# The routing of a top-2 expert layer moved ahead of its stage, and four stage beginnings put in another order, in a kernel of four transformer layers

## What is computed

```python
x = x + L0_xattn(layernorm(x), ctx)   # 16 heads of 8
x = x + L0_ffn(layernorm(x))          # 8 experts, argmax of 8 router scores, GELU, F = 512
x = x + L1_xattn(layernorm(x), ctx)   # 16 heads of 64
x = x + L1_ffn(layernorm(x))          # dense, piecewise linear GELU
x = x + L2_xattn(layernorm(x), ctx)   # self attention, GELU block, cross attention, GELU block
x = x + L2_ffn(layernorm(x))          # 8 experts, top 2:
...
logits = silu(xt @ rw1 + rb1) @ rw2 + rb2
_, idx = top_k(logits, 2)
w = softmax(where(mask_of(idx), logits, -inf))
h = silu(einsum('nd,edh->enh', xt, we1) + be1)
y = xt + einsum('ne,end->nd', w, einsum('enh,ehd->end', h, we2) + be2)
...
x = x + L3_xattn(layernorm(x), ctx)   # 16 heads of 8
x = x + L3_ffn(layernorm(x))          # 8 experts, argmax, GELU
```

## Time and profile before

| what | us |
|---|---|
| median of 3 runs (lowest, highest) | 1477.28 (1472.34, 1477.69) |
| profiled execution: its time, its span | 1477.49, 1475.7 |
| PE busy, share of the span | 1002.4, 68% |
| PEld (weight loads) | 753.7, 51% |
| DVE | 906.7, 61% |
| ACT | 696.9, 47% |
| POOL | 621.5, 42% |
| DMA | 71.57 MB, mean 49 GB/s |

### The profile page before, as it was taken

One profiled execution on the slowest core, in us unless ns is written; L12 is line 12 of the kernel. 1 busy time (PEld: TensorE's weight loads), 2 busy tenths in 40 slices (PEclk: granted clock), 3 DMA queues, 4 the chain that ended last, 5 costly groups with the idle time before them and its releaser, 6 DMA issues.

```text
span 1475.7 us, 37422 instructions
## 1 busy us (share of the span) xinstructions
PE 1002.4 (68%) x14883; PEld 753.7 (51%) x14940; DVE 906.7 (61%) x2386; ACT 696.9 (47%) x1404; POOL 621.5 (42%) x575
## 2 busy tenths in 40 slices
PE   1477578679898463678887478958259674567664
PEld 0355367446677243356664256735147462455554
DVE  4567554677775794788975567746244255766532
ACT  3556345565554432654526356645135354455321
POOL 3456723164353332364541355621440417556232
PEclk9778688889999675788987769968569795778787
DMA  6433222110010100000001000000212114431122
GB/s 198 132 95 108 69 68 63 40 40 24 23 31 10 34 17 32 19 16 10 3 3 36 1 2 3 4 2 1 69 37 72 42 36 115 137 111 44 48 73 72
DMA packets 68792, 71.57 MB, mean 49 GB/s; under 512 B 11599, under 2 KB 51919, under 8 KB 68431
## 3 DMA queue, kind: packets, MB, share of 16 engines
q1 hardware_dynamic: 64528, 60.78, 14.3%
q0 software_dynamic: 4096, 8.40, 1.8%
HBM read 44.91 MB, written 23.59 MB: 46 GB/s over the span
## 4 chain that ended last, share of the span: by engine, by line
PE 44%; DVE 22%; ACT 11%; issue 10%; POOL 6%; DMA 3%; POOLq 2%; SPq 1%; another core or an unknown queue 1%; ACTq 0%; DVEq 0%
PE psum L651 16%; PE psum L1132 6%; PE psum L1150 6%; DVE area L1742 4%; PE psum L773 2%; ACT xn L1243 2%; PE psum L813 2%; ACT area L1221 2%; PE psum L658 2%; DVE area L1862 2%; POOL sorted_in L2606 2%; DVE stats L1723 1%; POOLq L2416 1%; POOL area L2524 1%; DVE area L1848 1%
## 5 line engine op out<-in xcount | busy, mean ns | idle before, releaser
L1221 ACT ACTIVATE area<-psum 128x512 bf16<-128x512 f32 (+4 forms) x278 | 144.8, 541 | 239.6 <-PE psum L813 138.6
L1742 DVE TENSOR_TENSOR area<-psum,area 128x512 bf16<-128x512 f32 (+3 forms) x270 | 159.9, 620 | 58.1 <-ACT area L1221 52.0
L2335 DVE TENSOR_TENSOR area<-area 128x512 bf16<-128x512 f32 x106 | 73.7, 698 | 143.3 <-ACT area L1638 99.7
L2477 POOL TENSOR_TENSOR area<-area 77x1024 bf16<-77x1024 f32 x64 | 119.9, 1890 | 79.2 <-ACT area L1354 79.2
L1132 PE MATMUL psum<-xT_hi,moe 128*128 128x128 bf16 x848 | 114.6, 237 | 27.7 <-issue 23.7
L1150 PE MATMUL psum<-moe,area 128*128 x1272 | 110.9, 229 | 26.9 <-issue 25.9
L658 PE MATMUL psum<-wide,xn 128*128 128x128 f32 x144 | 32.7, 372 | 120.4 <-ACT xn L1243 108.4
L1354 ACT ACTIVATE area<-psum 77x1024 f32<-77x1024 f32 (+1 forms) x96 | 92.7, 1017 | 31.3 <-PE psum L773 31.3
L1150 PEld LDWEIGHTS psum<-moe,area 128*128 128x128 bf16 x1272 | 86.4, 102 | 40.9 <-issue 31.0
L2435 POOL TENSOR_TENSOR moe<-stage,moe 128x512 bf16<-128x512 f32 x47 | 55.6, 1183 | 120.7 <-ACT moe L1216 120.5
L1132 PEld LDWEIGHTS psum<-xT_hi,moe 128*128 x848 | 83.3, 107 | 37.2 <-issue 30.8
(11 more groups left out here) (245 smaller groups left out, 3010.2 us busy)
## 6 DMA issues: line engine op xcount, KB each, us to landing
area<-keys_dram SPq DMA_DIRECT2D x24, 320.0 KB, 4.8
area<-sorted_in SPq DMA_DIRECT2D x22, 256.0 KB, 3.4
sorted_out<-area SPq DMA_DIRECT2D x22, 256.0 KB
keys_dram<-area SPq DMA_DIRECT2D x8, 640.0 KB, 2.9
stage<-in_w_L0m SPq DMA_DIRECT2D x16, 256.0 KB
stage<-in_w_L2m SPq DMA_DIRECT2D x16, 256.0 KB
stage<-in_w_L3m SPq DMA_DIRECT2D x16, 256.0 KB
area<-queries_dram SPq DMA_DIRECT2D x24, 128.0 KB, 2.5
```

The source lines that it names most:

```text
L1221: ins = act.activation(out, bank, ACT.Copy)
L1742: ins = dve.tensor_tensor(out, bank, high, ALU.subtract)
L2335: dve.tensor_tensor(R.HL[u], R.HF[u], upper(R.HF[u]), ALU.subtract).then_inc(K.tile_split, tiles.one())
L2477: pool.tensor_tensor(A.PL[n % 4][0:A.L], A.PF[n % 4][0:A.L, :].rearrange("p (h q) -> p h q", h=8), A.PH[n % 4][0:A.L], ALU.subtract).then_ ...
```

## The change

Areas. VX and the maxima lie elsewhere in Dense's area, `VX_words` is the same memory as VX in words of 4 bytes, and the sorted rows of the late half lie behind the area of the results. `begun` says how many groups of an attention have their statistics from the stage in front: 2 in L1x and L3x, 1 in L0x, 0 in L2a1 and L2a2. `then` of L0m and L2m is now the attention behind them; `add_at`, `moments_at` and `shift_at` are tiles of the Routed loop.

```diff
+LATE_ROWS_AT = {1: OWN_AT + 2 * HB * D + 320, 2: OWN_AT + 2 * HB * D}
...
+        self.begun = 2 if late is not None else 0
...
+        self.begun = 2 if late is not None else 1
...
+        values = [words(GB * DENSE_TILES * 72) for _ in range(2)]
+        self.VX = [v.bitcast(BF16).rearrange("p (a n) -> p a n", a=2) for v in values]
+        self.VX_words = values
+        self.NM = [words(64, BF16) for _ in range(2)]
+        self.ON = [words(128).rearrange("p (h d) -> p h d", h=H) for _ in range(2)]
+        self.OT = words(128, BF16).rearrange("p (a n) -> p a n", a=2)
...
-        self.tiles = [K.carve(at, NT * D).rearrange("p (t d) -> p t d", d=D) for at in (AREA - D - NT * D, 0)]
+        self.tiles = [K.carve(at, NT * D).rearrange("p (t d) -> p t d", d=D)
+                      for at in (AREA - D - NT * D, LATE_ROWS_AT[k])]
+
+        self.then = None
+        self.add_at, self.moments_at, self.shift_at = (2 * NT - 8, 2 * NT - 4), 2 * NT - 3, 2 * NT - 1
```

```diff
         before, after = A.first_jobs()
+        if A.begun:
+            group_turned(0)
...
+        group_turned(0)
         project_keys(0)
-        group_turned(0)
...
-            if N.then is not None and g == 3:
-                for r in (0, 1):
-                    tokens_turned(N.then, r)
-        if N.then is not None:
-            for r in (0, 1):
+        for half in range(HALVES if N.then is not None else 0):
+            for r in (2 * half, 2 * half + 1):
+                tokens_turned(N.then, r)
+            for r in (2 * half, 2 * half + 1):
                 router_hidden(N.then, r)
-            for r in (0, 1):
+            for r in (2 * half, 2 * half + 1):
                 logits(N.then, r)
-            sort_half(N.then, 0)
+            sort_half(N.then, half)
...
-        if R.k == 2:
-            for g in (2, 3):
-                tokens_turned(R, g)
-            for g in (2, 3):
-                router_hidden(R, g)
-            for g in (2, 3):
-                logits(R, g)
-            sort_half(R, 1)
+        load_experts(0)
```

```diff
+    def table_loaded(fn):
+
+        i = stages.n
+        act.activation(K.table_of[:, i:i + 1], K.col("half"), fn)
...
+        normed(K.L0x.name, K.L0x.residual, 0)
...
-            sem.wait_ge(K.results_saved[1], A.late.saved)
+        table_loaded(ACT.Exp)
...
+            elif A.late is not None:
+                sem.wait_ge(K.results_saved[1], A.late.saved)
...
+        if A.begun:
+            group_turned(0)
...
+        group_turned(0)
         keys_hi(0)
+        head_rows(0)
+        queries_hi(0)
         repeat_keys(0)
-        head_rows(0)
-        normed(name, A.residual, 0)
         for t in range(1, 4):
             head_rows(t)
-        group_turned(0)
-        queries_hi(0)
...
+        table_loaded(ACT.Gelu)
...
-            if N.then is not None and g == 3:
-                for r in (0, 1):
-                    tokens_normed(N.then, r)
-                sem.wait_ge(K.affine_split, N.affine0 + NG)
-                for r in (0, 1):
-                    tokens_turned(N.then, r)
             for n in K.loads_of(name, g):
                 split_weights(n)
         if N.then is not None:
             for r in (0, 1):
-                router_hidden(N.then, r)
-            for r in (2, 3):
                 tokens_normed(N.then, r)
+            sem.wait_ge(K.affine_split, N.affine0 + NG)
+            for half in range(HALVES):
+                for r in (2 * half, 2 * half + 1):
+                    tokens_turned(N.then, r)
+                for r in (2 * half, 2 * half + 1):
+                    router_hidden(N.then, r)
+                if half == 0:
+                    for r in (2, 3):
+                        tokens_normed(N.then, r)
+            gates()
...
+        table_loaded(R.act_fn)
...
-        if R.k == 2:
-            for g in (2, 3):
-                tokens_turned(R, g)
-            for g in (2, 3):
-                router_hidden(R, g)
-            gates()
-        else:
+        if R.k == 1:
             tokens_normed(R, 3)
+        if R.b1 is not None:
+            load_experts(0)
...
+        if R.then is not None:
+            normed(R.then.name, R.then.residual, 0)
```

```diff
+        sem.wait_ge(K.load_first, 16)
+        first = norm_stats(K.L0x.residual, 0)
...
+        shift_of(0, first)
+        spread_masks(K.L0x)
...
-        g_stats(0)
         before, after = A.first_jobs()
+        if A.begun:
+            number["x", 1] = second_norm[name]
+            group_turned(0)
...
+        if A.begun < 2:
+            g_stats(1)
...
-            sem.wait_ge(K.values_zeroed, A.order + 1)
+            sem.wait_ge(K.values_zeroed, 2 * A.order + u + 1)
...
-                sem.wait_ge(K.values_zeroed, A.order + 1)
+                sem.wait_ge(K.maxima_zeroed, A.order + 1)
...
-        spread_masks()
-        g_stats(0)
+        group_turned(0)
         keys_lo(0)
         mask_keys(0)
-        shift_of(0, number[0])
-        group_turned(0)
         queries_lo(0)
...
-            for r in (0, 1):
-                route(N.then, r)
+            route(N.then, 0)
             for r in (2, 3):
                 shift_of(r, routed_norm[N.then.name, r])
+            route(N.then, 1)
             sort_half(N.then, 0)
+            for r in (2, 3):
+                route(N.then, r)
+            sort_half(N.then, 1)
+            gates()
...
-        if R.k == 2:
-            route(R, 2)
-            route(R, 3)
-            sort_half(R, 1)
-            gates()
...
-            if tile == HALVES * NT - 1:
-                for g in range(NG // HALVES):
-                    add_own(R, g)
+            if tile in R.add_at:
+                add_own(R, R.add_at.index(tile))
+            if R.then is not None and tile == R.moments_at:
+                sem.wait_ge(K.own_added, own_added.n)
+                number["first"] = norm_stats(K.x, 0)
+                second_norm[R.then.name] = norm_stats(K.x, 1)
+                if R.k == 2:
+                    spread_masks(R.then)
+            if R.then is not None and tile == R.shift_at:
+                shift_of(0, number["first"])
```

```diff
+        rstd(slice(0, 128), group(0))
...
-            pool.memset(A.NM[u], 0.0)
-            ins = pool.memset(A.VX[u].rearrange("p a n -> p (a n)"), 0.0)
-        ins.then_inc(K.values_zeroed, 1)
-        rstd(slice(0, 128), group(0))
+            ins = pool.memset(A.NM[u], 0.0)
+        ins.then_inc(K.maxima_zeroed, 1)
+        for u in range(2):
+            pool.memset(A.VX_words[u], 0.0).then_inc(K.values_zeroed, 1)
         prepare_sort(A.then)
         if A.late is not None:
...
+            if b < B and b % GB == 0:
+                late_values_lo(b // GB)
             if A.late is not None and b == 0:
                 gather(A.late, 3)
-            if b < B and b % GB == 0:
-                late_values_lo(b // GB)
...
+        if R.then is not None:
+            rstd(slice(0, 128), group(0))
+            rstd(slice(0, 128), group(1))
```

```diff
+        keys_away(0)
+        queries_away(0)
+        keys_back(0)
+        queries_back(0)
...
+    K.L0m.then, K.L2m.then = K.L1x, K.L3x
```

134 lines of the change are left out of this document (69 added, 65 removed).

## The result

The changed kernel takes 1429.89 us, the median of 4 runs (1424.11 to 1433.95), the kernel before 1474.81; the ratio is 0.9695 (95% interval 0.9650 to 0.9739). 1430 was forecast. Beside the experiments the same pair gave 1432.61 against 1477.8 (0.9697, 0.9671 to 0.9724), and on another chip 1431.32 against 1478.93 (0.9684, 0.9663 to 0.9705). The profiled execution took 1429.39, its span is 1427.6.

A forecast was written before the change was run, and what follows sets the result against it. No engine bounds it; twelve serial stages, each behind a border where every engine waits, do. Terms -16.7 - 13.0 - 10.2 - 6.8 - 3.6 - 0.8 + 3.9 = -47.2 from the profiled 1477.49 us gave 1430; range 1414 to 1447.

The forecast's parts named there:

- L2f2 to L2m: Border into L2m: second half's routing moves beside L2f2's scatter, second scatter starts at the border; -16.7 us, bounds -9 and -20.
- the lesser of the two shifts, that of the scatter: L2m's start: gain taken from the second scatter's earlier issue, 14.2 us, rather than from the first expert product's shift.
- Rival B: L2m's expert loop is not held by the scatter and runs on; another 11 us go, 1419 us; chance 0.08.
- 20 us of it under 22 us of cover: L2f2's end: 20 us of second-half routing fits beside GpSimd's 22 us scatter, with none of it on GpSimd.
- routing in L2f2 outlasted the scatter: Sign of being wrong: in L2f2 the moved routing ends later than GpSimd's scatter; no size given.
- rival A: L2f2's routing starves beside the scatter; the border gives 5 us instead of 16.7, 1442 us; chance 0.12.
- L2m to L3x: Border into L3x: border 2.9 us sooner, shorter starting chain and memsets, GpSimd's gathers decide; -13.0 us, bounds -8 and -16.
- keeps its length: L3x: add_own(3) behind GpSimd's gathers still takes 8.92 us.
- Start to L0x: Start and L0x's beginning: start some 2 us longer, first scores at 39.8 instead of 50.04; -10.2 us, bounds -7 and -13.
- rival D: Whole kernel slower: denser work lowers TensorE's granted clock; a mean of 0.73 gives 1490 us; chance 0.02.
- L0m to L1x: L1x's start: first maxima at 282.8 instead of 290.19, GpSimd's gathers early; -6.8 us, bounds -4 and -8.
- Tables: ScalarE's table loads moved to stage starts: three attentions give -3.6 us, three feed-forwards 0.8 more; bounds 0 and -6.

The follow-up runs named there:

- e2: Changed kernel with the second half's routing put back behind L2m's border: 1440.83 us.
- e5: Kernel before, unchanged, traced again: 1472.86 us, one run; its second theory was that something of the change, kept when L0x's old order returns, lengthens L0x's loop.
- e6: Changed kernel with VX cleared as bf16 again instead of f32 words: 1440.04 us.
- e7: Changed kernel with L1x not begun in L0m (L1x normalises its first group itself, early statistics taken out): 1444.8 us.
- e8: Changed kernel with every L2m tile using expert 0's weights and biases at a constant address: 1415.93 us.
- e3: Changed kernel with start and L0x put back into the order of before, L3x as changed: 1444.55 us.
- e4: Changed kernel without the small activations that load ScalarE's table at a stage's start: 1437.82 us.
- e10: Changed kernel with sort preparation moved behind gather(3) and the second VX cleared by VectorE in L3x: 1432.29 us.
- e9: Changed kernel run again unedited, as base for later runs on the same chip: 1431.32 us.

## Why the prediction came out right, and where its steps did not

**L2f2 to L2m (-16.7, and 2.9 of the next).** Measured -17.8 for both stages. The scatter of L2f2 starts 3.0 us sooner (2.5 forecast), the second scatter starts at the border, the first product comes at 4.8 (5). The tenth tile of the expert loop stands 38.0 us behind the border instead of 53.2, by VectorE's splits in the timelines: 15.2 to the forecast's 14.2; e2 puts it back to 53.2. Taking "the lesser of the two shifts, that of the scatter" was the decision that mattered. It was right on two of three chips. On the third TensorE is not held, and by the forecast's own working 15.5 us (20.5 less 5) would come; the kernel before has no trace there, so that is argued and not shown. Rival B's mechanism, a loop that the scatter doesn't hold, is real on one chip of three. Whether the holding on the other two is a wait of the kind that the rule quoted at rival B denies, no run tells.

The step that failed is the cover: "20 us of it under 22 us of cover" takes the routing to be as fast beside the scatter as in the open. From `route` to the last gate it took 13.0 us in the open (before, e5, e2) and 18.9 to 22.6 us in the ten traces that have it beside the scatter on these chips. In nine of the ten VectorE's drain is the last at the border, 0.4 to 3.9 us behind GpSimd's; "routing in L2f2 outlasted the scatter" was one of the forecast's signs of being wrong. That is where L2f2 fell short: 76.2 and 76.4 us with the routing 0.4 late, which is the forecast's -2.5, and 78.4 with it 2.6 late. So rival A's mechanism is real, and its price (11.7 us over the forecast) was not paid, since the cover was nearly long enough.

**L2m to L3x (-13.0).** First scores come 9.9 us sooner, the gathers end 9.7 sooner relative to the border and at 28.8 us of it (28.4 by the forecast's sum). L3x gains 13.1 where 10.1 were expected: 11.1 at the first exponentials (35.5 to 24.5) and the rest in the loop. One step that failed is that add_own(3) behind it, 8.92 us, "keeps its length": it took 6.68, 6.58 and 5.07 in the three traces. By e6 each microsecond of the gathers is worth 1.0 to 1.3 in the stage. The rest of the excess is within what the stage varies by: e7 and e8 have the same L3x and took 154.1 and 152.9. The memset at 0.85 ns a value was right: 0.86 for f32.

**Start to L0x (-10.2).** The beginning went as worked out: first scores at 16.4 us of the stage (15.3 forecast), start 1.7 longer (2 forecast). e3, which undoes it, costs 11.9 in the median and 9.8 in the stages. Against the traces of before, only 3.4 were to be seen. Of the 6.8 missing, 1.3 are that the first weights landed later in the three traces of the changed kernel (first copy at 14.5 on average against 13.2), 0.5 the beginning, and 5.0 L0x's loop. That is a step that the forecast did not have: L0x's loop runs at whatever clock TensorE is granted, and that differs between executions. Of twelve traces of kernels with a change in them, three at 0.81 have loops of 109.6 to 110.3 us, nine at 0.72 to 0.76 have 111.6 to 113.4; the two of before had 0.79 and 0.83 and 107.8 and 108.6. The loop of e3, with the old beginning, is long too (112.8 at 0.74), so the new order at the beginning is not what lengthens it. The clock explains some 2.5 us. Beside the three at 0.81 the two loops of before are still about 1.5 us shorter; why, no run settles (theory 2 of e5 is open), nor why the clock was low in nine of twelve. Of rival D, that denser work lowers the clock, there is no sign in the whole span: 0.804 against 0.798. In this one loop it is not excluded. The forecast's argument against D, that the lowest clocks stand in the stretches with little work, rests on L3x's start (0.51); L0x's start of before, as idle, had 0.98 and its busy middle 0.74.

**L0m to L1x (-6.8).** First maxima at 11.7 to 13.1 us (12 forecast), first exponentials 9.8 sooner (36.0 to 26.2); e7 gives 7.7 of these to early normalising and leaves 2.1 to the table and what else leads up to them. Both terms were a little small, by 0.9 each.

**Tables (-3.6 and -0.8).** The sum is near (e4: 5.2 in the median), its parts are not. L2a2 gains 2.5, L2a1 0.4, L1f and L2f1 nothing. The forecast let the load run behind the border, in ScalarE's wait; in the traces it runs ahead of the border, without the wait of the activation that needs it. So it costs nothing there.

**L0m and L3m begin later (+3.9).** Measured +1.5 in all; the first products stand 1.1 us further from the border in each. The step "the table (1.5) stands ahead of it" is wrong for that same reason; the register load remains.

So the forecast hit 1430 by luck as well, because errors cancelled: start and L0x gave 6.8 us less than their term, L2f2 and L2m 2.1 less, the feed-forwards 1.0 less; L3x gave 3.0 more, L1x 1.8, L2a1 and L2a2 0.5, and the late beginnings cost 2.4 less. The other half of the luck is the kernel before, whose median lay at 1474.8 with one more run.

## What to carry to other kernels

Work that a border holds back is worth moving ahead of it when another engine's queue already covers that time, but count what it waited for besides: here the next transfer decided (14 us), not the work that left (20 us). And don't take the work's length in the open for its length under the cover: here 13 us became 19 to 23, and the cover was outlasted. Price an early part by undoing it in the changed kernel, with the changed kernel beside it in the same group (e6 to e8 lacked it, and 2.4 us of drift looked like effect), and read the stages: two traces of the same loop differed by up to 3.8 us with the granted clock and by 2.8 us by when a first load landed, which is more than several of the terms. Later and sooner are not the same question: a delay of GpSimd's gathers cost 1.0 to 1.3 us for each one, while the run that brought them forward (e10) moved other work too and gained nothing.

## What the runs showed of the hardware

- On two chips of three TensorE issues, in the loops over expert tiles, many products only some 0.7 us apart while GpSimd issues indirect DMAs: 63 and 84 products in 21 us. The gaps begin 4 to 14 us after the first of these DMAs and end 1 to 3 us after the last. The third chip issued 207 and 264. With constant addresses (e8) the gaps stay, so register arithmetic is not their cause; what it is was not found. L2m took 138.4 us on the two and 107.8 on the third; that the gaps are all of the 31 us between is not shown.
- It is not TensorE alone: the small steps of the routing on VectorE and ScalarE take 18.9 to 22.6 us beside the scatter, 13.0 in the open and 13.4 beside it on the third chip. And it is not every indirect DMA: beside L3x's gathers TensorE ran 17 products in 2.2 us (e9).
- With constant addresses a tile takes 1.63 us, with addresses from registers 2.05: 0.42 us for some 17 operations on TensorE's registers and a few on ScalarE's.
- A table load (1283 ns) runs before the semaphore wait of the activation that needs it: 6 us ahead of the border in L0m.
- A memset goes by the value on GpSimd: 4.87 us for 5760 bf16 (e6), 2.47 for 2880 f32 over the same bytes. VectorE takes 2.46 for the latter.
- Casts with broadcast inputs on VectorE take 0.36 us alone and 3.4 to 5.3 beside a memset of GpSimd.
